# Third attention of a four-layer kernel: scores of a tile in four row groups of 32, value products of a batch's two units together

## What is computed

```python
qh = (q @ Wq.T).reshape(N, S_, HEADS, HEAD_DIM).transpose(0, 2, 1, 3)
kh = (k @ Wk.T).reshape(N, S_, GROUPS, HEAD_DIM).transpose(0, 2, 1, 3)
vh = (v @ Wv.T).reshape(N, S_, GROUPS, HEAD_DIM).transpose(0, 2, 1, 3)
kh = jnp.repeat(kh, GROUP_HEADS, axis=1)
vh = jnp.repeat(vh, GROUP_HEADS, axis=1)
score = jnp.einsum('bhqd,bhkd->bhqk', qh, kh) / math.sqrt(HEAD_DIM)
attn = jax.nn.softmax(score, axis=-1)
out = jnp.einsum('bhqk,bhkd->bhqd', attn, vh)
out = out.transpose(0, 2, 1, 3).reshape(N, S_, EMBED)
return out @ Wfc.T + bfc
```

## Time and profile before

| what | value |
|---|---|
| median of three runs | 1101.11 us (1100.45 to 1102.65) |
| span of the profiled execution, first to last instruction | 1099.8 us |
| TensorE busy | 900.0 us, 82% |
| VectorE busy | 777.1 us, 71% |
| ScalarE busy | 607.1 us, 55% |
| GpSimd busy | 441.5 us, 40% |
| mean granted TensorE clock | 0.925 |

### The profile page before, as it was taken

How to read it: one execution, slowest core, us unless ns; L and a number is a source line. 1 busy time by engine, 2 the same in 40 slices (tenths; PEclk the granted TensorE clock), 3 DMA queues, 4 the chain that set the end, 5 groups by cost and what they waited for, 6 DMA issues and landing times.

```text
span 1099.8 us, 20339 instructions
## 1 busy us (share of the span) xinstructions
PE 900.0 (82%) x5861; PEld 673.8 (61%) x5861; DVE 777.1 (71%) x2020; ACT 607.1 (55%) x1385; POOL 441.5 (40%) x518
## 2 busy tenths in 40 slices
PE   5867969977999875788879899986899999963486
PEld 3556859976777634444456555644778888732354
DVE  6756637967888677888768887755856455389885
ACT  3663337764444258799835556666235655431764
POOL 3175634541000012677435545441037777706000
PEclk9978989997999988999969999999999999965699
DMA  9943546758200011222191002002025533360001
GB/s 267 184 152 118 182 152 213 231 167 284 77 20 6 1 54 48 55 75 75 63 300 31 11 11 67 1 20 87 1 69 177 156 128 98 96 215 0 1 25 53
DMA packets 95971, 109.19 MB, mean 99 GB/s; under 512 B 14269, under 2 KB 85842, under 8 KB 95874
## 3 DMA queue, kind: packets, MB, share of 16 engines
q1 hardware_dynamic: 84162, 76.76, 23.6%
q0 software_dynamic: 11712, 31.20, 8.9%
HBM read 73.89 MB, written 34.03 MB: 98 GB/s over the span
## 4 chain that ended last, share of the span: by engine, by line
PE 45%; DVE 13%; POOL 11%; issue 8%; ACT 7%; DMA 3%; SPq 0%; ACTq 0%; DVEq 0%; POOLq 0%
PE bank L3346 4%; PE bank L2768 3%; PE bank L1584 3%; POOL f_outputs L2095 2%; PE bank L2809 2%; POOL f_got L2087 2%; PE bank L1610 2%; PE bank L3372 2%; POOL f_got L3124 2%; PE bank L2802 2%; POOL f_outputs L3130 2%; PE bank L1903 2%; DVE resid L1000 2%; PE bank L1928 2%; PE bank L3723 1%
## 5 line engine op out<-in xcount | busy, mean ns | idle before, releaser
L3124 POOL DMA_INDIRECT f_got<-f_tokens,f_places x54 | 53.6, 992 | 64.0 <-DVE f_places L946 47.8
L3256 DVE TENSOR_TENSOR f_act<-f_silu,bank 128x256 f32<-128x256 f32 x54 | 22.8, 421 | 63.5 <-ACT f_silu L3173 62.2
L1284 POOL DMA_INDIRECT f_outputs<-f_y,f_places x39 | 41.6, 1066 | 56.6 <-ACT f_y L1334 35.0
L3130 POOL DMA_INDIRECT f_outputs<-f_y,f_places x54 | 54.7, 1014 | 22.9 <-issue 11.6
L2522 POOL TENSOR_TENSOR work<-work 128x512 f32<-128x512 f32 x32 | 32.7, 1053 | 71.1 <-ACT work L2572 71.1
L2087 POOL DMA_INDIRECT f_got<-f_tokens,f_places x39 | 38.1, 976 | 54.6 <-DVE f_places L946 37.7
L2670 DVE TENSOR_REDUCE work<-bank 128x8 f32<-128x512 f32 x64 | 43.4, 678 | 12.4 <-PE bank L2768 12.2
L2095 POOL DMA_INDIRECT f_outputs<-f_y,f_places x39 | 40.5, 1038 | 23.2 <-ACT f_y L2150 15.0
L3173 ACT ACTIVATE f_silu<-bank 128x256 f32<-128x256 f32 x54 | 20.7, 384 | 52.6 <-PE bank L3346 52.6
L2674 DVE TENSOR_TENSOR work<-bank,work 128x512 f32<-128x512 f32 x64 | 44.3, 692 | 3.7 <-ACT work L2634 1.6
L2634 ACT ACTIVATE work<-work 128x512 f32<-128x512 f32 x64 | 40.3, 630 | 7.3 <-DVE work L2674 7.2
(11 more groups left out here) (557 smaller groups left out, 3144.4 us busy)
## 6 DMA issues: line engine op xcount, KB each, us to landing
f_back<-f_outputs SPq DMA_DIRECT2D x21, 256.0 KB, 4.9
f_back<-f_outputs SPq DMA_DIRECT2D x10, 512.0 KB, 6.4
f_got<-f_sorted SPq DMA_DIRECT2D x39, 129.0 KB
f_sorted<-clear_row SPq DMA_DIRECT2D x1, 4992.0 KB, 25.1
raw<-in_L_ffn_w SPq DMA_DIRECT2D x24, 176.0 KB
tern_raw<-in_L_ffn_gate_w SPq DMA_DIRECT2D x8, 512.0 KB, 5.7
tern_raw<-in_L_ffn_up_w SPq DMA_DIRECT2D x8, 512.0 KB, 4.2
tern_raw<-in_L_ffn_down_w SPq DMA_DIRECT2D x8, 512.0 KB, 5.8
```

The costliest lines, as they stand in the source:

```text
L1284: pool.indirect_dma_start(g.outputs, bass.IndirectOffsetOnAxis(ap=dest[:, j:j + 1], axis=0), y_out[:, j % OUT_RING, :], None).then_inc(gon ...
L3124: pool.indirect_dma_start(got[:, j % GATHERS, :], None, tokens, bass.IndirectOffsetOnAxis(ap=sorter.token[:, j:j + 1], axis=0)).then_inc(s ...
L3130: pool.indirect_dma_start(outputs, bass.IndirectOffsetOnAxis(ap=sorter.dest[:, j:j + 1], axis=0), y_out[:, j % OUT_RING, :], None).then_in ...
```

## The change

Scores: the 64 rows of a pair are cut into two halves of 32 rows (four groups each). kblk has 4 x 64 = 256 columns, with a mask `in_half` that tells the four groups of a half. A batch's scores are four matmuls of 32 rows x 256 columns, one per pair and half, each in a row group and a bank of its own: unit x % 2 has bank pair SOFT[x % 2], the half picks the bank in it, the batch of the tile the left or right 256 columns. One call of `tensor_scores` makes the scores of a tile (eight matmuls), at the end of step x % 4 = 1 for the tile that starts at x + 3, after `shifted` has reached all units before it. VectorE reads a unit from two banks in one instruction; score has four buffers; attended and residual come one step later. The value products of both units of a batch stand together at even steps; at odd steps the turn of prob waits for probT itself. READ moves from bank 5 to 6.

```diff
@@ -90,7 +90,8 @@
-        bank = [ctx.enter_context(nc.psum_tensor(f"bank{i}", [P, 512], F32)) for i in range(8)]
+        bank_pair = [ctx.enter_context(nc.psum_tensor(f"bank{2 * i}{2 * i + 1}", [P, 2, 512], F32)) for i in range(4)]
+        bank = [bank_pair[i // 2][:, i % 2, :] for i in range(8)]
...
@@ -2411,12 +2412,14 @@
-            kblk = lay(QB, GROUPS, SEQ)
+            HALVES, HALF = 2, GROUPS // 2
+            kblk = lay(QB, HALF, SEQ)
             vblk = lay(SLOTS, SC, 2 * AUG)
-            score, prob, probT = lay(2, GROUPS * SEQ), lay(2, GROUPS * SEQ), lay(2, GROUPS * SEQ)
+            SCORES = 2 * PAIRS
+            score, prob, probT = lay(SCORES, GROUPS * SEQ), lay(2, GROUPS * SEQ), lay(2, GROUPS * SEQ)
...
-            SOFT, IN, TURN, READ, OUT = (bank[0], bank[1], bank[4], bank[6]), bank[2], bank[3], bank[5], bank[7]
+            SOFT, IN, TURN, READ, OUT = (bank_pair[0], bank_pair[2]), bank[2], bank[3], bank[6], bank[7]
...
+
+            def soft(x):
+
+                at = x // PAIRS % 2 * HALF * SEQ
+                return SOFT[x % PAIRS][:, :, at:at + HALF * SEQ]
...
-                sp.wait_ge(s.score, UNITS // PAIRS)
+                sp.wait_ge(s.score, UNITS // TILE_U)
...
+                pool.tensor_tensor(in_half, in_group[:, 0:HALF], in_group[:, HALF:GROUPS], ALU.add).then_inc(s.group, 1)
+                pool.wait_ge(s.group, 5)
...
-                    n = [P, GROUPS, SEQ]
+                    n = [P, HALF, SEQ]
...
                         if not isinstance(h, int) or h:
-                            pool.wait_ge(s.score, h * QB + b - QB + 1)
-                        pool.tensor_tensor(kblk[:, b], kT[:, b, :].unsqueeze(1).to_broadcast(n), in_group.unsqueeze(2).to_broadcast(n),
+                            pool.wait_ge(s.score, (h * QB + b - QB) // 2 + 1)
+                        pool.tensor_tensor(kblk[:, b], kT[:, b, :].unsqueeze(1).to_broadcast(n), in_half.unsqueeze(2).to_broadcast(n),
                                            ALU.mult).then_inc(s.kblk, 1)
...
-                        act.activation(prob[:, x % 2, :], score[:, x % 2, :], ACT.Exp, scale=HD ** -0.5).then_inc(s.exp, 1)
+                        act.activation(prob[:, x % 2, :], score[:, x % SCORES, :], ACT.Exp, scale=HD ** -0.5).then_inc(s.exp, 1)
...
-                        got = SOFT[x % 4][:, :].rearrange("p (g k) -> p g k", g=GROUPS)
-                        dve.wait_ge(s.score, nth(i, x, BATCH_U) + 1)
-                        dve.tensor_reduce(top[:, x % 2, :], got, AX.X, ALU.max).then_inc(s.top, 1)
+                        got = soft(x).rearrange("p h (g k) -> p h g k", g=HALF)
+                        dve.wait_ge(s.score, nth(i, x, TILE_U) + 1)
+                        dve.tensor_reduce(top[:, x % 2, :].rearrange("p (h g) -> p h g", h=HALVES), got, AX.X, ALU.max).then_inc(s.top, 1)
                         dve.wait_ge(s.top, U + 1)
-                        if not isinstance(i, int) or x >= 2:
-                            dve.wait_ge(s.exp, U - 1)
-                        dve.tensor_tensor(score[:, x % 2, :].rearrange("p (g k) -> p g k", g=GROUPS), got,
-                                          top[:, x % 2, :].unsqueeze(2).to_broadcast([P, GROUPS, SEQ]), ALU.subtract).then_inc(s.shifted, 1)
+                        if not isinstance(i, int) or x >= SCORES:
+                            dve.wait_ge(s.exp, U - SCORES + 1)
+                        dve.tensor_tensor(score[:, x % SCORES, :].rearrange("p (h g k) -> p h g k", h=HALVES, g=HALF), got,
+                                          top[:, x % 2, :].rearrange("p (h g) -> p h g", h=HALVES).unsqueeze(3).to_broadcast([P, HALVES, HALF, SEQ]), ALU.subtract).then_inc(s.shifted, 1)
...
-                    if x % 4 == 0 and inside(i, x - 8, UNITS):
-                        t = nth(i, x - 8, TILE_U)
+                    if x % 4 == 1 and inside(i, x - 9, UNITS):
+                        t = nth(i, x - 9, TILE_U)
...
-                    if x % 4 == 2 and inside(i, x - 10, UNITS):
-                        t = nth(i, x - 10, TILE_U)
+                    if x % 4 == 3 and inside(i, x - 11, UNITS):
+                        t = nth(i, x - 11, TILE_U)
...
-                for x in range(UNITS + 10):
+                for x in range(UNITS + 11):
...
             def tensor_scores(pe, i, x):
 
-                slot = x // PAIRS % SLOTS
                 if isinstance(i, int) and x < PART:
-                    if x % TILE_U == 0:
-                        hold(pe, s.qT, x // TILE_U + 1)
+                    hold(pe, s.qT, x // TILE_U + 1)
                 elif x % PART == 0:
                     hold(pe, s.qT, nth(i, x, PART) + 2)
-                hold(pe, s.kblk, nth(i, x, BATCH_U) + 1)
-                if not isinstance(i, int) or x >= 4:
-                    hold(pe, s.shifted, i * ROUND + x - 2)
-                for pair in range(PAIRS):
-                    rows = slice(pair * GD, (pair + 1) * GD)
-                    mm = pe.matmul(SOFT[x % 4 + pair][:, :], qT[rows, slot, :], kblk[rows, slot % QB].rearrange("p g k -> p (g k)"),
-                                   start=True, stop=True)
+                hold(pe, s.kblk, nth(i, x, BATCH_U) + 2)
+                if not isinstance(i, int) or x >= TILE_U:
+                    hold(pe, s.shifted, i * ROUND + x)
+                for b in range(2):
+                    slot = (x // PAIRS + b) % SLOTS
+                    for pair in range(PAIRS):
+                        for half in range(HALVES):
+                            at = pair * GD + half * HALF * HD
+                            rows = slice(at, at + HALF * HD)
+                            mm = pe.matmul(soft(2 * b + pair)[:, half, :], qT[rows, slot, :], kblk[rows, slot % QB].rearrange("p g k -> p (g k)"),
+                                           start=True, stop=True, skip_group_check=True)
                 mm.then_inc(s.score, 1)
...
                 for e in range(PT):
                     tensor_first_queries(pe, e)
-                    tensor_scores(pe, 0, 2 * e)
+                    if e == 0:
+                        tensor_scores(pe, 0, 0)
 
                 def step(i, x):
-                    if inside(i, x - 1, UNITS):
-                        slot, pair = (x - 1) // PAIRS % SLOTS, (x - 1) % PAIRS
-                        B = nth(i, x - 1, BATCH_U)
+                    if x % 2 == 0 and inside(i, x - 2, UNITS):
+                        slot, B = (x - 2) // PAIRS % SLOTS, nth(i, x - 2, BATCH_U)
                         hold(pe, s.probT, i * ROUND + x)
-                        if pair == 0 and (not isinstance(B, int) or B):
+                        if not isinstance(B, int) or B:
                             hold(pe, s.readT, B)
-                        for c in range(SC):
-                            mm = pe.matmul(READ[c * 2 * AUG:(c + 1) * 2 * AUG, pair * P:(pair + 1) * P], vblk[:, slot, c, :],
-                                           probT[:, (x - 1) % 2, c * P:(c + 1) * P], start=True, stop=True, skip_group_check=True)
-                        if pair == PAIRS - 1:
-                            mm.then_inc(s.readT_ps, 1)
+                        for pair in range(PAIRS):
+                            for c in range(SC):
+                                mm = pe.matmul(READ[c * 2 * AUG:(c + 1) * 2 * AUG, pair * P:(pair + 1) * P], vblk[:, slot, c, :],
+                                               probT[:, pair, c * P:(c + 1) * P], start=True, stop=True, skip_group_check=True)
+                        mm.then_inc(s.readT_ps, 1)
                     if inside(i, x, UNITS):
+                        if x % 2 == 1:
+                            hold(pe, s.probT, i * ROUND + x)
                         hold(pe, s.exp, i * ROUND + x + 1)
                         for c in range(SC):
                             tp = pe.transpose(TURN[:, c * P:(c + 1) * P], prob[:, x % 2, c * P:(c + 1) * P], ident[:, :])
                         tp.then_inc(s.probT_ps, 1)
-                    if x % 2 == 1 and inside(i, x + 3, UNITS):
-                        tensor_scores(pe, i, x + 3)
                     if x % 4 == 1 and inside(i, x - 5, UNITS):
                         t = nth(i, x - 5, TILE_U)
                         hold(pe, s.readT, 2 * nth(i, x - 5, TILE_U) + 2)
@@ -2834,6 +2846,8 @@
                         layer2_entry.tensor(pe, *ENTRY_TURNS[x])
                     if x % PART < 4 and inside(i, x + PART, UNITS):
                         tensor_stages[x % PART](pe, nth(i, x, PART) + 1, (x // PART + 1) % 2)
+                    if x % TILE_U == 1 and inside(i, x + 3, UNITS):
+                        tensor_scores(pe, i, x + 3)
                 over_units(pe, step, 10)
```

More of the change, by code:

```diff
@@ L2413, in layer2_attention @@
             kT = lay(QB, SEQ)
-            kblk = lay(QB, GROUPS, SEQ)
+            HALVES, HALF = 2, GROUPS // 2
+            kblk = lay(QB, HALF, SEQ)
             vblk = lay(SLOTS, SC, 2 * AUG)
```

(5 more changed lines are left out.)

## The result

The change makes the kernel slower: 1109.65 us (median of 13 runs) against 1100.96, a ratio of 1.0085 with a 95% interval of 1.0065 to 1.0105. Forecast were 1095.2 us and a gain.

The account below looks back on a forecast made before the run. TensorE was taken as the bound, busy 20.83 of a 22.49 us round. Start +1.3, combine rounds -0.4, others -6.0, norms +1.6, end -2.4 gave -5.9: 1101.1 to 1095.2 us; range 1087 to 1109, likeliest 1092 to 1099.

Parts of the forecast that it names:

- Scores: TensorE's scores of a tile in four row groups: 1.04 to 1.06 us, saving 2.3 us per round.
- Rival 2: Scores' four row groups run together only by twos: +13.6 - 5.9 = +7.7, 1108.8 us; chance 0.10.
- Value products: Both units of a batch in one TensorE step: 0.57 us in place of 2 x 0.36; 1.2 us a round.
- The ground of the sum: TensorE's work falls from 20.8 to 17.3 us a round, worth 5 a round if nothing took its place.
- Start: First tile's scores at half clock, then scores 4 to 7 waiting until unit 3 is shifted: +1.3 us.
- Stretches A and B: A, step-1 scores to step-5 turn of readT: 9.75 us; B, step-5 scores to next step-1 turn of readT: 7.0.
- the walk: One round summed: 9.75 + 7.0 + 3.7 = 20.4 us against 22.4; with one combine in B, no gain.
- with its two waits for TURN and the one for att: In stretch B TensorE takes 6.9 us including these waits, VectorE 7.0, so VectorE or both set B.
- Three rounds with combines: -0.4: Attention rounds in which VectorE also runs the earlier layer's combine: -0.4 us for the three together.
- Three without: -6.0: Attention rounds after the combines end, 20.4 us against 22.4 each: -6.0 us for the three together.
- Tail: Last scores done at step 57, turn goes through at once: -2.4 us; next norm's means and shifts: +1.6.
- rival 3: The single set of score banks costs more, through VectorE: at 1.2 us per round +3.5, 1104.6 us; chance 0.17.

Follow-up runs that it names:

- the change with the filler: The changed kernel plus ten useless identity transposes on TensorE at x % 8 = 7, before the wait for attended: 1102.83 us, 1.0003 of the kernel before.
- the old order with late places: The kernel before with only VectorE's attended and residual one step later (x % 4 = 1 and 3): 1110.15 us, 1.0083.

## Why the prediction was wrong

*Scores.* Right. 1.07 us a tile from start to start (685.59 to 686.66), predicted 1.04 to 1.06; four row groups of 32 do run together. Rival 2 falls. A record of 32 rows and 256 columns lasts 0.374 here, where one of 64 and 512 lasted 0.589, 0.215 less, for the 0.213 of the sum. That the 0.10 is weight load was an estimate: the runs show only that the first records last 0.10 longer, in both kernels.

*Value products.* Right, 0.58 (690.96 to 691.54) for 0.57.

*The ground of the sum.* It counts a microsecond of TensorE's work as one of the round, less what takes its place; that rests on the earlier trace rows. In the round from 676.17 its busy time fell by 2.7 us (20.83 to 18.15) and the round by 1.2 (22.5 to 21.3).

*Start.* Predicted +1.3, measured +1.5 to the second keys stage and +0.9 to the third.

*Stretches A and B.* At clock 1.00 with no combine the walk holds. A: from the value products at 675.10 to the turn of readT at 684.95, 9.85 us, predicted 9.75. B: 686.66 to 693.93, 7.3 for 7.0. That round takes 21.3 in place of 20.4: 0.4 of the difference lies in A and B, the rest between them (4.2 for 3.7), where the tokens stage now waits for ScalarE's copy of the context turned just before (0.21 in this round, up to 0.39 in others).

*The step that failed* is the sentence that TensorE needs 6.9 in B "with its two waits for TURN and the one for att", and the sum built on it: "Three rounds with combines: -0.4. Three without: -6.0." I had sized the wait for attended once, in a round where no combine and no late norms stand before it, and let VectorE's chain alone carry them. The wait then came out at 0.7 to 3.5 us, and in the sum the clock was taken as 1.00 throughout these rounds. Measured: +4.4 for the three rounds of the first term, and +1.2 for the three of the second (23.7, 21.3 and 23.4 for 22.4, 22.5 and 22.4). The chain wait for attended, halved clock, turn, value products, turn, product with wfT, residual, turn of readT, scores is the path there. Filling 1.25 us of the wait, with attended no earlier, gives back 8.1 of 9.2 us.

*A count in the same sum* was wrong as well. Of the "three without" combines only two are without. VectorE's timeline of the kernel before, in the round from 645.18 to 667.60:

```profile
645.59 1.00 DVE L2285 SCALAR_TENSOR_TENSOR resid<-f_back,f_places,resid 128x256 f32<-128x256 f32 x2
...
656.24 1.00 DVE L2285 SCALAR_TENSOR_TENSOR resid<-f_back,f_places,resid 128x256 f32<-128x256 f32 x2
...
663.15 1.00 DVE L2285 SCALAR_TENSOR_TENSOR resid<-f_back,f_places,resid 128x256 f32<-128x256 f32 x2
```

The last is the combine of unit 34, which stands in stretch B. By the walk's own rule that round gains nothing, so -6.0 should have been -4.0 and the forecast about 1097. That alone doesn't turn the sign.

*Tail.* Predicted -2.4 for the last scores and +1.6 for means and shifts; measured +1.4 from the last keys stage on, at clock 0.85 (0.96 before). That the halved clock took the gain at the last scores is likely, but argued from the windows only; no run separates it.

*The rivals.* The time is 0.65 us beyond the range's end, on rival 3's side: the single set of banks does cost what the scores save (1.0009 alone). Norms and combines between a tile's scores and the next are also rival 3's; but it let them act through VectorE's chain alone. The wait for attended and the clock behind it are on none of my lists.

What stays open is why value products per unit take away most of the loss while attended is still late (1.0024). The clock is part of it. Windows from the second keys stage to the last residual, in this order: the kernel before, the change, the change with the filler, the change with products per unit:

```profile
576.42:757.73 181.31, 159.78 (x1285) 102.12 (x1284) 136.62 (x260) 110.21 (x234) 84.38 (x98) 0.99 0.11 33
```

```profile
579.25:767.58 188.33, 148.27 (x1393) 113.00 (x1392) 135.65 (x260) 110.59 (x234) 71.71 (x98) 0.92 0.10 31
```

```profile
578.80:763.60 184.80, 152.84 (x1473) 118.96 (x1472) 135.54 (x260) 110.38 (x234) 71.76 (x98) 0.94 0.10 31
```

```profile
569.30:751.60 182.30, 149.40 (x1393) 108.95 (x1392) 135.42 (x261) 109.96 (x234) 71.80 (x98) 0.94 0.11 35
```

Without the merging the clock comes back by as much as with the filler, from 0.92 to 0.94, and in the tail above all: there it is 1.00 (736.00 to 751.60) where the change has 0.81 (740.00 to 767.58); in the rounds ahead of it both have 0.93. But that is 8 us less at half clock, an estimate of some 3 us of work, of the 6 by which the stage is shorter, and each is a single execution (the last one the fastest of its twelve). Why the clock falls less often there, no run shows. Open is also, in the old order with late places, how its 9 us divide between waits and clock.

## What to carry to other kernels

When an edit leaves TensorE less work, look at where its idle time collects, not only at how much there is. A wait can cost more than its own length: behind the longest one here the next steps ran at half the clock and took 5.7 us in place of 3.4, in the loop. Look at the granted clock behind each wait. Test two small edits together as well as apart: late places and merged products cost 0.85% together in the new order and little with either one undone. When buffers are cut to one set, every block between two refills of the consumer is on the path: move what can wait into the time in which that engine stands idle, and what others wait for ahead of it.

## What the runs showed of the hardware that was not expected

Ten useless transposes (1.25 us) in a wait made the kernel 8.1 us faster. The longest wait left behind them, 2.4 us, was still followed by a stretch at 0.50 (619.50 to 622.50). In the changed kernel two stretches at 0.50 set in within or right behind a long wait of TensorE: from 616.70 and from 644.00 us on, the first in the wait of 3.46 us that ends at 618.18, the second where one of 3.12 us ends at 644.04. But the wait for attended before the stretch from 668.00 is only 0.71 us, and an idle time of 0.51 follows it. How long or how frequent idle time must be for it, these runs don't show.
